# Expert routing by quarters of the tokens, with slots gathered by indirect transfers, in a two-layer mixer kernel on one Trainium2 core

## The reference

```python
xn = _layernorm(x)
s = _L0_attn_ref(xn, ...)
logits = xf @ Wg + bg                       # xf: the 8192 tokens of xn, 8 experts
one_hot = jax.nn.one_hot(jnp.argmax(logits, axis=-1), 8)
h = jax.nn.gelu(jnp.einsum('td,edh->eth', xf, W1), approximate=True)
y = jnp.einsum('eth,ehd->etd', h, W2)
out = jnp.einsum('etd,te->td', y, one_hot)  # the chosen expert alone
x = x + s * _silu(out)
x = x + _L1_attn_ref(_layernorm(x), ...) * _silu(_L1_ffn_ref(_layernorm(x), ...))
```

## Time and profile before

| | |
|---|---|
| median of 3 runs | 3473.93 us (3471.63 to 3474.02) |
| profiled execution | 3440.83 us, its span 3439.0 us |
| TensorE busy | 3112.3 us, 90% of the span |
| VectorE, ScalarE, GpSimd busy | 72%, 68%, 37% |
| opening | from 0 to 370.4 us of the span |

### The profile page before, as it was taken

How to read it: one execution, slowest core, us unless ns; L and a number is a source line. 1 busy time by engine, 2 the same in 40 slices (tenths; PEclk the granted TensorE clock), 3 DMA queues, 4 the chain that set the end, 5 groups by cost and what they waited for, 6 DMA issues and landing times.

```text
span 3439.0 us, 83502 instructions
## 1 busy us (share of the span) xinstructions
PE 3112.3 (90%) x34007; PEld 1889.5 (55%) x34008; DVE 2466.9 (72%) x5000; ACT 2338.7 (68%) x4758; POOL 1261.4 (37%) x799
## 2 busy tenths in 40 slices
PE   5589799999999999999999999999999999999976
PEld 5168445556564646555565656565555656464644
DVE  6432487868687877878676868778786868687643
ACT  1265467777777786777767776867777777778744
POOL 1622034333333443444333333444443333344343
PEclk9889899999999999999999999999999999999987
DMA  6256110101011111101011111111010101111000
GB/s 190 69 160 187 48 28 14 32 27 38 27 28 31 34 31 34 31 16 33 23 36 29 28 31 34 31 34 31 15 35 22 38 27 28 34 31 31 5 13 4
DMA packets 130458, 138.95 MB, mean 40 GB/s; under 512 B 17972, under 2 KB 112542, under 8 KB 129566
## 3 DMA queue, kind: packets, MB, share of 16 engines
q1 hardware_dynamic: 120368, 104.77, 11.2%
q0 software_dynamic: 9712, 28.85, 2.9%
HBM read 80.87 MB, written 35.39 MB: 34 GB/s over the span
## 4 chain that ended last, share of the span: by engine, by line
PE 46%; DVE 21%; ACT 9%; POOL 6%; issue 4%; DMA 2%; SPq 2%; POOLq 0%; ACTq 0%; DVEq 0%
PE bank L1882 5%; PE bank L1319 4%; DVE turn_f L2056 4%; PE bank L698 4%; PE bank L1926 3%; ACT prob_a L1388 3%; PE bank L1303 3%; PE bank L1332 3%; DVE nmax_a L1443 3%; PE bank L1868 3%; PE bank L1858 2%; PE bank L1849 2%; DVE ss L2049 2%; DVE nmax_f L2063 2%; POOL turn_f L1797 2%
## 5 line engine op out<-in xcount | busy, mean ns | idle before, releaser
L1388 ACT ACTIVATE prob_a<-bank 128x512 f32<-128x512 f32 x1024 | 564.4, 607 | 190.0 <-PE bank L1332 185.2
L1443 DVE TENSOR_REDUCE nmax_a<-bank 128x1 f32<-128x512 f32 x768 | 502.5, 684 | 161.6 <-PE bank L1303 160.5
L1791 POOL TENSOR_TENSOR rn<-ss,minus_half 128x16 f32<-128x16 f32 x128 | 377.8, 2952 | 270.6 <-DVE ss L2051 268.6
L1814 POOL TENSOR_TENSOR rs_f<-rs_f,minus_half 128x4 f32<-128x4 f32 x32 | 32.6, 1018 | 1108.2 <-DVE rs_f L1181 1108.2
L1797 POOL TENSOR_TENSOR turn_f<-turn_f 128x512 f32<-128x512 f32 x256 | 324.3, 1287 | 207.7 <-DVE turn_f L2056 207.7
L1332 PE MATMUL bank<-Qst_a,Kst_a 74*128 74x512 bf16 x1024 | 378.9, 389 | 18.9 <-ACT prob_a L1388 9.5
L1944 ACT ACTIVATE area<-bank 128x512 f32<-128x512 f32 x640 | 349.9, 603 | 63.2 <-PE bank L1882 55.2
L2056 DVE TENSOR_TENSOR turn_f<-area,rotf 128x1024 f32<-128x1024 f32 x256 | 307.6, 1219 | 8.7 <-POOL area L1801 6.2
L1303 PE MATMUL bank<-Kst_a,Qst_a 72*128 72x512 bf16 x768 | 302.2, 394 | 5.4 <-DMA Kst_a<-dk_a 1.2
L1319 PE MATMUL bank<-prob_a,V_a 128*9 128x512 f32 x2048 | 274.5, 609 | 13.2 <-ACT prob_a L1388 11.8
L1801 POOL TENSOR_TENSOR area<-turn_f,rn 128x1024 f32<-128x1024 f32 x128 | 267.5, 2090 | 19.0 <-POOL turn_f L1797 0.9
(11 more groups left out here) (288 smaller groups left out, 7007.4 us busy)
## 6 DMA issues: line engine op xcount, KB each, us to landing
Qst_a<-dq_a SPq DMA_DIRECT2D x192, 96.0 KB
Kst_a<-dk_a SPq DMA_DIRECT2D x192, 96.0 KB
dq_a<-prob_a SPq DMA_DIRECT2D x80, 128.0 KB
dk_a<-prob_a SPq DMA_DIRECT2D x48, 128.0 KB
area<-xs_d SPq DMA_DIRECT2D x39, 128.0 KB, 4.3
ys_d<-otok_f SPq DMA_DIRECT2D x39, 128.0 KB, 1.9
x_a<-in_x_in SPq DMA_DIRECT2D x16, 256.0 KB, 2.8
xs_d<-turn_f SPq DMA_DIRECT2D x4, 1024.0 KB, 9.9
```

Source lines behind the costliest of these rows:

```text
L1388: nc.scalar.activation(dst, bk.full(act, product)[0:rows, :], func, **kw).then_inc(a_emptied["act"], 1)
L1443: nc.vector.tensor_reduce(out=nmax_a[:, g, t, j:j + 1], in_=bk.full(dve, f)[:], op=ALU.max, axis=AX.X, negate=True).then_inc(emptied, 1)
L1791: nc.gpsimd.tensor_tensor(rn[:, t % 2], ss[:, t % 2], minus_half[:], ALU.pow).then_inc(f_root, 1)
```

## The change

- No zero fill. `xs_d` has 8192 rows, one a token, in place of 9984 slots. Its rows are ordered by quarter of the tokens (four rows of x, 2048 tokens), then by expert, then by token.
- After each quarter's logits DVE chooses its experts (`choose`), PE sums the ranks inside the quarter in PSUM by 23 bf16 products (`ranks`), and DVE has the rows (`rows_of`). POOL scatters the quarter's 16 tiles then.
- When all quarters are counted, DVE works out the counts, the blocks' experts, for each of 9984 slots the row of `xs_d` that holds its token (`m_slots`), and last each token's slot `pos`.
- Blocks fetch their slots with two indirect gathers of 128 rows on POOL (`slots`), not with one plain load on SP.
- The table `OPEN` is new throughout the opening. The tables of `rows` are as they were.

The diff, cut to its core (the number tables, the tile declarations and the pool's last waits are left out):

```diff
         def open_sync(sp):
...
                              (tri[:], consts["tri"]), (block_at[:], consts["block_at"]), (part_off[:], consts["part_off"]),
+                             (expert_key, consts["expert_key"]),
+                             (quarter_row, consts["quarter_row"].rearrange("p (c e) -> p c e", e=NX)),
+                             (slot_at, consts["slot_at"].rearrange("p (j c) -> p j c", c=ST)),
...
-            for at in fills:
-                n = min(4 * T, SLOTS * E // P - at)
-                sp.dma_start(rows[:, at:at + n], zeros[:, 0:n]).then_inc(m_filled, 16)
...
-                if j + XS < NBLK:
-                    sp.dma_start(slot_ring[:, (j + XS) % XS], slot_rows(xs_d, j + XS)).then_inc(m_xs[j % XS], 16)
...
         def open_gpsimd(pool):
...
-            pool.wait_ge(m_pos, 2)
-            for j in range(WS_EARLY):
-                weights(j)
-            for n in range(TILES):
-                nc.gpsimd.indirect_dma_start(
-                    out=xs_d, out_offset=bass.IndirectOffsetOnAxis(ap=pos[:, n:n + 1], axis=0),
-                    in_=x_tile(n), in_offset=None).then_inc(m_sorted, 16)
...
+            def slots(j):
+                for c in range(ST):
+                    nc.gpsimd.indirect_dma_start(
+                        out=slot_ring[:, j % XS, c], out_offset=None, in_=xs_d,
+                        in_offset=bass.IndirectOffsetOnAxis(ap=m_slots[:, j, c:c + 1], axis=0)).then_inc(m_xs[j % XS], 16)
...
+            yield 38
+            pool.wait_ge(m_pos, 1)
+            sort(range(0, 6))
+            yield 46
+            inverse_root(3)
+            sort(range(6, 16))
+            for c in range(1, 4):
+                yield 50 + 12 * c
+                pool.wait_ge(m_pos, c + 1)
+                sort(range(16 * c, 16 * c + 8))
+                if c == 3:
+                    yield 91
+                    pool.wait_ge(m_pos, 5)
+                    for j in range(WS_EARLY):
+                        weights(j)
+                yield 56 + 12 * c
+                sort(range(16 * c + 8, 16 * c + 16))
+            for j in range(NBLK):
+                yield block_slot(j - XS) - 1
+                if j == 0:
+                    pool.wait_ge(m_pos, 6)
                     pool.wait_ge(m_sorted, 16 * TILES)
+                if j >= XS:
+                    pool.wait_ge(m_slotT, j - XS + 1)
+                slots(j)
+                if j >= WS_EARLY:
+                    yield block_slot(j - XS) + 1
+                    if j >= WS:
+                        pool.wait_ge(m_y, j - WS + 1)
+                    weights(j)
...
+            def ranks(c):
+
+                pe.wait_ge(m_hot, c + 1)
+                ps, first = rank_bank(c), 16 * c
+                nc.tensor.matmul(ps, tri[:], hot_bf[:, first:first + 16, :], start=True, stop=False, skip_group_check=True)
+                for m in range(15):
+                    last = nc.tensor.matmul(ps[:, NX * (m + 1):].rearrange("p (n e) -> p n e", e=NX), ones_sq[:],
+                                            hot_bf[:, first + m:first + m + 1, :].to_broadcast([P, 15 - m, NX]),
+                                            start=False, stop=False, skip_group_check=True)
+                for e in range(NX - 1):
+                    last = nc.tensor.matmul(ps.rearrange("p (n e) -> p n e", e=NX)[:, :, e + 1:], ones_sq[:],
+                                            m_held[:, c, e:e + 1].unsqueeze(1).to_broadcast([P, 16, NX - 1 - e]),
+                                            start=False, stop=(e == NX - 2), skip_group_check=True)
+                last.then_inc(m_ranks, 1)
...
-            nc.vector.memset(turn_f[:], 0.0)
...
+            for at, step, c in ((14, normalise, 0), (18, statistics, 1), (22, normalise, 1), (26, statistics, 2), (30, choose, 0),
+                                (33, normalise, 2), (37, rows_of, 0), (38, statistics, 3), (43, choose, 1), (46, normalise, 3),
+                                (49, rows_of, 1), (53, choose, 2), (58, rows_of, 2), (62, choose, 3), (66, rows_of, 3)):
+                yield at
+                step(c)
...
+            for q in (0, 4):
+                link(nc.vector.tensor_tensor(weighed, m_cmp.unsqueeze(1).to_broadcast([P, 4, NBLK, NX]),
+                                             m_step[:, q:q + 4, :].unsqueeze(2).to_broadcast([P, 4, NBLK, NX]), ALU.mult))
+                link(nc.vector.tensor_reduce(out=m_picked[:, q:q + 4, :], in_=weighed, op=ALU.add, axis=AX.X))
...
+            nc.vector.tensor_scalar(m_slots, slot_at, 0.0, None, ALU.max).then_inc(m_pos, 1)
```

More of the change, by code:

```diff
@@ L711, in mixer_kernel @@
         m_att, m_attW = sem("m_att"), sem("m_attW")
-        m_early, m_filled, m_x = sem("m_early"), sem("m_filled"), [sem(f"m_x{c}") for c in range(4)]
+        m_early, m_x = sem("m_early"), [sem(f"m_x{c}") for c in range(4)]
         m_var, m_rstd, m_xn, m_dve = sem("m_var"), sem("m_rstd"), sem("m_xn"), sem("m_dve")
@@ L822, in open_sync @@
             sp.dma_start(rotary, consts["rotary"].rearrange("p (a t d) -> p a t d", a=4, d=FD)).then_inc(s_weights, 16)
-            for j in range(-XS, NBLK):
-                if j >= 0:
-                    yield block_slot(j) + 9
+            for j in range(NBLK):
+                yield block_slot(j) + 9
                 if j == 2:
@@ L838, in open_gpsimd, with inverse_root, sort @@
         def open_gpsimd(pool):
-            for c in range(4):
-                yield 15 + 7 * c
+            def inverse_root(c):
                 pool.wait_ge(m_var, c + 1)
                 nc.gpsimd.tensor_tensor(m_rs[:, c % 2, 1, :], m_rs[:, c % 2, 0, :], m_half[:], ALU.pow).then_inc(m_rstd, 1)
+            def sort(tiles):
+                for n in tiles:
+                    nc.gpsimd.indirect_dma_start(
+                        out=xs_d, out_offset=bass.IndirectOffsetOnAxis(ap=m_row[:, n:n + 1], axis=0),
+                        in_=x_tile(n), in_offset=None).then_inc(m_sorted, 16)
             def weights(j):
@@ new lines, in open_gpsimd @@
+            for c in range(3):
+                yield 15 + 7 * c
+                inverse_root(c)
+            yield 38
[15 more added lines that the diff above has]
+                sort(range(16 * c + 8, 16 * c + 16))
@@ new lines, in open_gpsimd @@
+            for j in range(NBLK):
+                yield block_slot(j - XS) - 1
+                if j == 0:
+                    pool.wait_ge(m_pos, 6)
+                    pool.wait_ge(m_sorted, 16 * TILES)
+                if j >= XS:
[6 more added lines that the diff above has]
+                    weights(j)
@@ L891, in open_tensor @@
                     row_logits(r - 1)
+                if r % 4 == 1 and r > 4:
+                    yield 22 + 2.5 * r
+                    ranks(r // 4 - 1)
             row_logits(B - 1)
             yield 67.5
-            pe.wait_ge(m_hot, 1)
+            ranks(3)
             pe.wait_ge(m_tout, B)
-            hots = hot_bf.rearrange("p n e -> p (n e)")
-            nc.tensor.matmul(banks[4][:], tri[:], hots, start=True, stop=True)
-            nc.tensor.matmul(banks[5][:], ones_sq[:], hots, start=True, stop=True).then_inc(m_ranks, 1)
+            for c in range(4):
+                last = nc.tensor.matmul(banks[5][:, NX * c:NX * (c + 1)], ones_sq[:], m_held[:, c, :], start=True, stop=True)
+            last.then_inc(m_ranks, 1)
             def slots_T(j):
-                pe.wait_ge(m_xs[j % XS], 16 * (j // XS + 1))
+                pe.wait_ge(m_xs[j % XS], 16 * ST * (j // XS + 1))
                 if j:
@@ L931, in open_tensor @@
             yield block_slot(0) - 1
-            pe.wait_ge(m_pos, 1)
+            pe.wait_ge(m_pos, 6)
             slots_T(0)
@@ new lines, in open_vector @@
+            yield 68
+            dve.wait_ge(m_ranks, 5)
+            link(nc.vector.tensor_copy(m_sum, banks[5][:, 0:4 * NX].rearrange("p (c e) -> p c e", e=NX)))
+            nc.vector.memset(m_cum[:, 0, :], 0.0)
+            link(nc.vector.memset(m_low[:, :, 0:1], 0.0))
+            for c in range(3):
+                link(nc.vector.tensor_tensor(m_cum[:, c + 1, :], m_cum[:, c, :], m_sum[:, c, :], ALU.add))
+            link(nc.vector.tensor_tensor(m_total, m_cum[:, 3, :], m_sum[:, 3, :], ALU.add))
@@ new lines, in open_vector @@
+            for c in range(3):
+                link(nc.vector.tensor_tensor(slots4, slots4, beyond[:, c:c + 1], ALU.add))
+            nc.vector.tensor_scalar(m_slots, slot_at, 0.0, None, ALU.max).then_inc(m_pos, 1)
+            link(nc.vector.tensor_tensor(m_off, m_off, base.to_broadcast([P, 4, NX]), ALU.subtract))
+            link(nc.vector.tensor_tensor(chosen.rearrange("p (c n) e -> p c n e", c=4), hot_bf.rearrange("p (c n) e -> p c n e", c=4),
+                                         m_off.unsqueeze(2).to_broadcast([P, 4, 16, NX]), ALU.mult))
@@ L1060, in slots_out @@
+            link(nc.vector.tensor_reduce(out=m_max, in_=chosen, op=ALU.add, axis=AX.X))
```

(2 more changed lines are left out.)

158 lines of the change are left out of this document (80 added, 78 removed), and 235 rows, old and new, of the table OPEN.

## The result

The changed kernel took **3526.14 us** (median of 4 runs, 3510.92 to 3531.07), the kernel before in the same comparison 3473.97 (3471.63 to 3482.16): ratio **1.0139, 95% interval 1.0103 to 1.0174**. It is 52 us slower where 10 us less were forecast, and outside the forecast's range (3449 to 3481).

The account below looks back on a forecast made before the run. PE was taken to stand still 36.7 us awaiting POOL's scattered slots, and to bound the blocks. Removing that, with maxima 16.5 us later, moved the opening's end from 370.4 to 360: 3473.9 − 10 = 3464 us, range 3449 to 3481.

Parts of the forecast that it names:

- the rest of the span I take as it is: Everything after the opening, which ends at 370.4 us: assumed to keep its time, since the change is confined to the opening.
- They are off the path: POOL's scatters beside the routing: from 49 to 139 us, slots there at 146, before PE's first slot transpose at 168.5.
- 33 us below the median ... I take the difference in time over.: Sum made on the profiled execution, 3440.8 us; its difference in time then applied to the runs' median, 3473.9.
- The opening's own working: Opening: its end moves from 370.4 to 360 us, a gain of 10 us.
- the term of the sum for the rank products: Logits stage on PE: 23 rank products at 0.123 us each, 2.8 us a quarter; bounds −6 to +11 us over all four.
- The end of the routing: Mostly DVE, after the last logits at 85: 25 us instead of 20, to 110, so attention's maxima begin 16.5 us later.
- Rival 1: Attention: PE's clock rises early, all three groups at the higher clock; −18 us, 3456; chance 0.17.
- two signs of being wrong: Opening, two of the named signs: attention's maxima before 103 (or after 117); products of 0.39 us before 140.
- Rival 3: Blocks: POOL becomes the bound if a gather costs over 1.5 us; gain gone, at 1.7 3477 to 3478; chance 0.13.
- The Trainium skill's rule: Blocks' gathers: software-built GpSimd descriptors are slower to set up, so blocks would be worse; the forecast took 1.25 us a gather.

Follow-up runs that it names:

- before_waits: The kernel before with 95 already satisfied waits on PE behind the last logits, chip 14: ratio 1.0031 (1.0012 to 1.0049).
- after_both_more: The changed kernel with an unused DRAM tensor (old scratch addresses) and 135 satisfied waits on PE, chip 3, 12 runs: 3425.24 us, ratio 0.9964.
- after_pad: The changed kernel with an unused tensor of 1792 rows putting ys_d, dq_a and dk_a at their old addresses, chip 14: ratio 1.0013 (0.9991 to 1.0035).
- after_third: The changed kernel, unchanged, profiled on the disturbed chip 8: 3515.75 us.
- after_more: The changed kernel, unchanged, on quiet chip 7, 12 runs: 3441.11 us, ratio 1.0001 (0.9983 to 1.0020).
- plain_slots: The changed kernel with one plain transfer per block on GpSimd's queue instead of two gathers, rows not the routed ones, chip 10: 3444.11 us, ratio 1.0002.
- before_third: The kernel before, unchanged, profiled on the disturbed chip 8: 3470.79 us.
- before_look: The kernel before, unchanged, profiled on quiet chip 7: opening 365.6 us, rows 2617.0 us.

## Why the prediction was wrong

- **The step that failed most: "the rest of the span I take as it is."** Code that the diff does not touch took 35 us longer on chip 8 (2654.6 against 2619.7), and in the profiles on quiet chips 23 and 29; by the ratio of all runs it is about 14 to 18 there, what the opening gains. On chip 8 that alone turns the forecast's −10 into +25. `before_waits` (ratio 1.0031) and `after_both_more` (0.9964, beside 1.0013 for `after_pad` on another chip) show from both sides that it comes with what stands in PE's list ahead of the rows, and not with what the opening computes.
- **The second: "They are off the path"**, of the scatters. In cost to POOL they are as forecast (0.96 + 0.30 each, first at 49.1, end of the last 139.4 on chip 7, forecast 49 and 139). On chip 8, from some 20 us on, a run of them holds PE, ACT, DVE and SyncE. Before, they ran beside attention, which had 37 us of slack; now they run beside the routing, which has none. On chip 8 the maxima begin 54.7 us later than before (145.67 against 90.98), forecast 16.5, and the blocks take 4.4 and not 3.78. The opening is 13.0 us longer there, where 10 less were forecast.
- **The sum for the first comparison**, in chip 8's numbers, where changed and before were both profiled: opening +13.0, to the first store −4.9, rows +34.9, rest +1.5: +44.6 (spans 3513.6 and 3469.0, one execution each), of 52 measured. The other 7 are open; the first comparison's own opening, 418.1, is 7 longer than `after_third`'s.
- **"33 us below the median ... I take the difference in time over."** It was the warning: 3440.83 lies outside the runs' own range, 3471.63 to 3482.16. The profile has all its landings and was of a quiet execution; the runs, by their times, were not. On chip 8 the same kernel has 3470.8 with 26 us of the difference in this very opening. The two first traces laid side by side would give the opening +46, where chip 8's pair has +13.
- **The opening's own working held on quiet chips**, with more gained than forecast: −14.2 to −18.2 against −10. Maxima begin at 100 and not at 110: the last logits stood at 76 and not at 85. About half of that is the term of the sum for the rank products, of which a set took 1.5 us at the lower clock and 1.0 at the higher, not 2.8. Rows of `after_more`:

```profile
43.40 1.03 PE L946 MATMUL bank<-mix_f,ones_sq 128*128 128x120 bf16 x15
44.29 0.59 PE L950 MATMUL bank<-xnT_f,ones_sq 128*128 128x112 bf16 x7
76.78 0.29 DVE L1084 TENSOR_TENSOR x_b<-bank,bg_s 128x128 f32<-128x128 f32 x1
100.12 1.28 DVE L1546 TENSOR_REDUCE nmax_a<-bank 128x1 f32<-128x512 f32 x2
...
333.42 0.42 DVE L1184 COPY otok_f<-bank 128x256 f32<-128x256 f32 x1 [1.36 <-PE bank L1005]
337.15 0.42 DVE L1184 COPY otok_f<-bank 128x256 f32<-128x256 f32 x1 [1.36 <-PE bank L1005]
```

  The end of the routing, 76.8 to 100.1, took 23.3 us where 25 were counted. The first slots are copied at 155.4 (forecast 168.5) with no wait for a DMA, the second hidden layer begins at 187.8 (197), and blocks follow at 3.73 to 3.74 from 229 on (3.78 from 220.5).
- **Rival 1 (clock early)** held in part: in `after_more` products are 0.38 to 0.39 us from 121.5 to 138.3 and again from 145.4, and 0.61 between. What it gave is inside the 14 to 18 us. The kernel before has such a stretch on chip 7 too (110.0 to 123.6), where its opening ends at 365.6; on chip 10, where it ends at 371.9, it has no product of 0.39 us before 147.6. With the maxima before 103 it is one of two signs of being wrong that the prediction named and that came on quiet chips, on the side of more gain.
- **Rival 3 (POOL bounds the blocks)** named the place and not the mechanism. A gather keeps its 0.94 us on chip 8; it is the neighbours that are late. `plain_slots` shows that gathers are free on a quiet chip (opening to 355.3 without them, 353.7 with them). Its price was also summed wrongly: by its own terms a gather of 1.7 us gives −10 + 16 − 7 + 14 = +13, 3487 and not 3477 to 3478, so that the range's upper end of 3481 does not follow from it.
- **The Trainium skill's rule** against this step ("DMA: Bandwidth & Descriptors", SWDGE vs HWDGE vs iDMA), that software-built descriptors are slower to set up, is not what hurt: on quiet chips blocks are 3.73 to 3.74 us apart with SyncE's plain loads, with plain loads from GpSimd's queue and with its gathers.

## What to carry to other kernels

A profile whose own time lies outside the range of the runs was taken under other conditions than they were: profile the kernel before again, beside the changed one, before a sum is made. A long run of indirect transfers from GpSimd belongs beside work that has slack; on one of five chips here it held up the other engines. When a change ahead of a long unrolled part loses what it gained, shift the later instructions by some satisfied waits and time that too, over all runs and not by one profile: here it cost one kernel 11 us and, with the unused tensor, gave the other 12.

## What the runs showed of the hardware

- On chip 8 and in the first comparison, once indirect transfers have run 1.26 us apart for some 20 us, instructions of PE, DVE and SyncE start on a step of 0.7 us and DVE's releases come up to 23 us late. Four us after the transfers paused in the first comparison's changed kernel all was normal (93.6 to 97.6); after the last weight load of `before_third` it took eight (182.3 to 190.2). On chips 10, 7, 14 and 3 the same stream does nothing of the kind. One transfer in 3.73 us does no harm on either. What in the chip does it was not found; hundreds of missing landings go with it.
- The granted-clock column can read 1.00 where the trace has no record of the clock. The first profile of the kernel before has its first record at 147.5 us, where products go from 0.61 to 0.39 us; ahead of it the 1.00 of the earlier trace rows stands for nothing, and products of 0.61 us say the lower level. `before_look` has records for the same stage, and there products change with the clock: half until 110.0, full for 13.6 us, then half again, with PE busy for 7.0 of 7 us from 102, 6.5 of 8 from 111 and 9.0 of 9 from 125.

```profile
100.00:134.00 34.00, 28.02 (x98) 6.13 (x98) 17.17 (x30) 15.39 (x26) 25.77 (x28) 0.70 0.22 70
109.46 0.63 PE L1303 MATMUL bank<-Kst_a,Qst_a 72*128 72x512 bf16 x1
110.02 0.39 PE L1332 MATMUL bank<-Qst_a,Kst_a 74*128 74x512 bf16 x1
123.76 0.61 PE L1303 MATMUL bank<-Kst_a,Qst_a 72*128 72x512 bf16 x1 [1.43 <-DMA Kst_a<-dk_a]
```

- 95 satisfied waits on an idle PE made the kernel 0.31% slower over ten runs (0.12% to 0.49%), though its opening is no longer (369.1 us).
